# Mixer scalings by one number per row on ScalarE, all step orders written anew, table loads ahead of waits

## The reference, cut to what matters

```python
x  = L0_attn_x
xn = layernorm(x); s = L0_mixer(xn); g = silu(fp4_ffn(xn));        x = x + s * g
xn = layernorm(x); s = L1_entmax_attention(xn); g = silu(moe8(xn)); x = x + s * g
xn = layernorm(x); s = L2_rotating_recurrence(xn); g = silu(moe8_bf16(xn)); x = x + s * g
xn = layernorm(x); s = L3_relative_attention(xn); g = silu(int8_ffn(xn)); x = x + s * g
```

```python
xdt   = x * dt                       # dt: one number per token and head
Acs   = cumsum(dt * A)
Y     = (C B^T * exp(Acs_l - Acs_s)) @ xdt + exp(Acs) * C @ state
state = exp(Acs_last) * state + B^T @ (exp(Acs_last - Acs) * xdt)
y     = rmsnorm((Y + D * x) * silu(z)) @ W_out
```

## Time and profile before

| what | value |
|---|---|
| median of 3 runs | 3212.22 us (3211.52 to 3215.06) |
| the profiled execution, its span | 3209.0 us, 3.2 us below the median |
| PE / DVE / ACT / POOL busy | 74% / 79% / 51% / 18% |
| first part: 44 to 1960 us | DVE busiest |
| second part: 1962 to 2232 us | PE busiest |
| attention of layer 3: 2300 to 3121 us | PE busiest |
| table loads on ACT | 94, of 1283 ns each |

### The profile page before, as it was taken

The page is one execution under the profiler, slowest core; times in us unless marked ns, Lnnn a source line. Parts: engine busy times, 40 slices in busy tenths (PEclk is TensorE's granted clock), DMA queues, the critical chain, the costliest instruction groups (busy, mean ns, idle before and its releaser), DMA issues.

```text
span 3209.0 us, 40003 instructions
## 1 busy us (share of the span) xinstructions
PE 2383.4 (74%) x13729; PEld 1300.2 (41%) x13729; DVE 2544.2 (79%) x5554; ACT 1633.2 (51%) x3182; POOL 565.8 (18%) x610
## 2 busy tenths in 40 slices
PE   3697876967958769679674304997688898888888
PEld 1333333333333333334331101332366676666663
DVE  3386898998999999989989673887577777777764
ACT  1344436245344353353442412666587888777862
POOL 0000300302203003012030020001332323323320
PEclk9698987977978879779777655999799999999999
DMA  2001100100101001001010004200688877888751
GB/s 73 1 22 43 30 25 28 35 32 23 34 29 30 26 24 33 28 27 31 30 24 23 23 8 123 57 9 31 198 226 223 235 222 225 220 215 227 220 157 43
DMA packets 270758, 265.92 MB, mean 83 GB/s; under 512 B 15224, under 2 KB 244235, under 8 KB 268987
## 3 DMA queue, kind: packets, MB, share of 16 engines
q1 hardware_dynamic: 270554, 263.37, 28.8%
HBM read 130.48 MB, written 124.45 MB: 79 GB/s over the span
## 4 chain that ended last, share of the span: by engine, by line
DVE 41%; PE 31%; ACT 14%; issue 9%; DMA 2%; POOL 2%; SPq 1%; DVEq 0%; POOLq 0%; ACTq 0%
PE banks L2642 5%; PE banks L2688 4%; DVE t L2618 3%; DVE t L1017 2%; PE banks L2602 2%; DVE t L1169 2%; ACT L144 2%; DVE t L952 1%; ACT t L2629 1%; PE banks L1085 1%; ACT t L2553 1%; DVE t L2673 1%; DVE t L1700 1%; DVE t L1704 1%; ACT t L1395 1%
## 5 line engine op out<-in xcount | busy, mean ns | idle before, releaser
L2618 DVE CUSTOM_DVE_ANT_0 t<-banks,t 128x640 f32<-128x640 f32 (+7 forms) x512 | 377.8, 747 | 135.2 <-PE banks L2642 62.2
L2629 ACT ACTIVATE t<-t 128x640 f32<-128x640 f32 (+7 forms) x512 | 391.0, 780 | 81.3 <-DVE t L2618 80.4
L2642 PE MATMUL banks<-ident,t 128*128 128x128 f32 x2304 | 360.1, 281 | 41.6 <-DVE t L2839 14.4
L2642 PEld LDWEIGHTS banks<-ident,t 128*128 128x128 f32 x2304 | 253.8, 142 | 108.1 <-ACT t L2629 50.5
L2602 PE MATMUL banks<-t 128*128 128x512 bf16 (+3 forms) x768 | 197.3, 333 | 39.4 <-DVE t L2618 37.5
L2583 POOL TENSOR_TENSOR t<-t 128x512 f32<-128x512 f32 x96 | 122.6, 1277 | 551.1 <-DMA t<-relative_scratch 455.7
L548 POOL TENSOR_TENSOR t<-t 128x512 f32<-128x512 f32 x28 | 48.1, 1718 | 915.7 <-ACT t L520 915.7
L2673 DVE COPY t<-banks 128x512 f32<-128x512 f32 x256 | 175.6, 686 | 32.2 <-PE banks L2642 31.3
L1085 PE MATMUL banks<-t 128*128 128x512 f32 x256 | 145.0, 650 | 42.9 <-DVE t L1165 32.3
L1740 ACT ACTIVATE t<-t 128x16 f32<-128x16 f32 x256 | 82.5, 322 | 184.1 <-DVE t L1704 142.4
L1119 ACT ACTIVATE t<-banks 128x512 f32<-128x512 f32 x128 | 76.4, 597 | 195.6 <-PE banks L1085 195.4
(11 more groups left out here) (453 smaller groups left out, 5956.2 us busy)
## 6 DMA issues: line engine op xcount, KB each, us to landing
relative_scratch<-t SPq DMA_DIRECT2D x128, 512.0 KB, 3.6
t<-relative_scratch SPq DMA_DIRECT2D x128, 512.0 KB, 5.2
relative_scratch<-t SPq DMA_DIRECT2D x128, 256.0 KB, 4.1
t<-in_wmoe SPq DMA_DIRECT2D x64, 384.0 KB, 3.0
t<-cut_scratch SPq DMA_DIRECT2D x192, 64.0 KB
t<-t SPq DMA_DIRECT2D x16, 512.0 KB, 4.2
cut_scratch<-t SPq DMA_DIRECT2D x8, 768.0 KB, 4.1
z_scratch<-t SPq DMA_DIRECT2D x8, 512.0 KB, 3.1
```

Of the source, the lines that this page charges most:

```text
L2618: nc.vector.tensor_tensor_reduce(s.s[z][:, 0:n], ps[:, b0:b0 + 1 + i // 4, :].rearrange("p b n -> p (b n)")[:, 0:n], s.bias[r][:, j, WIDE ...
L2629: nc.scalar.activation(s.s[z][:, 0:n], s.s[z][:, 0:n], ACT.Exp, scale=-1.0, bias=s.least[:, z:z + 1]).then_inc(*a.mark("weights", u))
L2642: nc.tensor.transpose(ps[:, 4 + c % 2, (t - lo) * P:(t - lo + 1) * P], s.s[u % NS][:, t * P:(t + 1) * P], k.ident[:]).then_inc(*e.mark("tu ...
```

## The change: what it does, and the diff

Four things change.

1. In the mixer, three scalings leave VectorE. `xdt` becomes four ScalarE copies (one per head, 64 columns, with a factor per partition), `xdd` four more, and the decayed state four more into a new buffer `kept`; VectorE's addition then reads `kept`. ScalarE's copy of B no longer waits for VectorE, but for TensorE. TensorE waits for `gated_low` of VectorE and `xdd` of ScalarE where it waited for `xdd` of VectorE and `btok`.
2. In all stages the call that may load a table stands ahead of the wait of its activation and no longer behind it.
3. All tables of letters but `TURNS_POOL` are new: those of PE, ACT, DVE and SP for the first part, and those of PE, ACT and DVE for the second part and the attention.
4. One more buffer of 128x256.

```diff
     yield
+    k.table(LOGEXP)
     act.wait_ge(e, "var", u)
-    k.table(LOGEXP)
...
@@ mixer_pe
-            pe.wait_ge(v, "xdd", u, t)
-            pe.wait_ge(a, "btok", u, t)
+            pe.wait_ge(v, "gated_low", u, t)
+            pe.wait_ge(a, "xdd", u, t)
             mm(o, s.xdt[:, h, :], s.low[:, h, :], start=True, stop=first).then_inc(*e.mark())
...
@@ mixer_act
     for t in range(NT):
         yield
-        act.wait_ge(v, "xdt", u, t)
+        act.wait_ge(e, "turned", u, t)
         nc.scalar.copy(s.btok[:], ps[:, 0, DI0:DI0 + P]).then_inc(*a.mark("btok", u, t))
+        yield
+        for h in range(H0):
+            nc.scalar.activation(s.xdt[:, h, :], ps[:, 0, h * HP:(h + 1) * HP], ACT.Copy, scale=s.dt[:, t, h:h + 1]).then_inc(
+                *a.mark("xdt", u, t))
...
         yield
+        k.table(LOGEXP)
         act.wait_ge(a)
-        k.table(LOGEXP)
         nc.scalar.activation(s.ec, bank(ps, 2).rearrange("p (h t) -> p h t", h=H0), ACT.Exp).then_inc(*a.mark())
...
         nc.scalar.activation(s.dd[:], s.dd[:], ACT.Exp).then_inc(*a.mark("decay", u, t))
+        yield
+        act.wait_ge(a)
+        for h in range(H0):
+            nc.scalar.activation(s.xdd[:, h, :], s.xdt[:, h, :], ACT.Copy, scale=s.dd[:, h:h + 1]).then_inc(*a.mark("xdd", u, t))
+        if u:
+            yield
+            if t:
+                act.wait_ge(v, "state", u, t - 1)
+            for h in range(H0):
+                nc.scalar.activation(s.kept[:, h, :], s.state[:, t, h, :], ACT.Copy, scale=s.ec[:, h, P - 1:P]).then_inc(
+                    *a.mark("kept", u, t))
...
@@ mixer_dve
-        yield
-        dve.wait_ge(e, "turned", u, t)
-        tt(s.xdt[:], ps[:, 0, 0:DI0].rearrange("p (h q) -> p h q", h=H0), rep(s.dt[:, t, :], 2, HP), ALU.mult).then_inc(*v.mark("xdt", u, t))
...
-        tt(s.low, s.low, rep(s.gm[:], 1, H0), ALU.mult).then_inc(*v.mark())
-        tt(s.xdd[:], s.xdt[:], rep(s.dd[:], 2, HP), ALU.mult).then_inc(*v.mark("xdd", u, t))
+        tt(s.low, s.low, rep(s.gm[:], 1, H0), ALU.mult).then_inc(*v.mark("gated_low", u, t))
...
-            tt(s.state[:, t], s.state[:, t], rep(s.ec[:, :, P - 1], 2, HP), ALU.mult).then_inc(*v.mark())
-            yield
-            dve.wait_ge(v)
-            tt(s.state[:, t], s.state[:, t], new, ALU.add).then_inc(*v.mark("state", u, t))
+            dve.wait_ge(a, "kept", u, t)
+            tt(s.state[:, t], s.kept[:], new, ALU.add).then_inc(*v.mark("state", u, t))
...
 TURNS_SP = (
...
-    "wwwwwwwwbxiiittwwbwwwwxiiittbb"
+    "wwwbwbiwitwwwiwwwxwtibittixbb"
 )
...
-        s.xdt, s.xdd, s.btok = sb([P, H0, HP]), sb([P, H0, HP]), sb([P, P])
+        s.xdt, s.xdd, s.kept, s.btok = sb([P, H0, HP]), sb([P, H0, HP]), sb([P, H0, HP]), sb([P, P])
```

More of the change, by code:

```diff
@@ L731, in ffn0_act @@
         yield
+        k.table(SILU)
         act.wait_ge(e, "gate", u, t)
-        k.table(SILU)
         nc.scalar.activation(f.hid[t // 2][:, t % 2], ps[:, S0, 0:FF0], ACT.Silu).then_inc(*a.mark("silu", u, t))
@@ L2153, in readout2_act @@
     yield
+    k.table(ROOT)
     act.wait_ge(e, "var", b)
-    k.table(ROOT)
     nc.scalar.activation(s.stat[:, 0], ps[:, 1, 0:2], ACT.Sqrt, bias=k.eps5[:]).then_inc(*a.mark("root", b))
@@ L2274, in moe2_act @@
     yield
+    k.table(SIGMOID)
     act.wait_ge(e, "logits", b)
-    k.table(SIGMOID)
     nc.scalar.activation(o.rb.score, ps[:, bb, 0:NT * E2].rearrange("p (t e) -> p t e", t=NT), ACT.Sigmoid).then_inc(
```

241 lines of the change are left out of this document (120 added, 121 removed).

## The result

The changed kernel takes 3206.06 us (median of 16 runs, 3201.09 to 3212.53), the kernel before, run beside it, 3214.76 us. The ratio is 0.9965, 95% interval 0.9954 to 0.9975: faster by 0.35%, which is 8.7 us by the two medians and 11 us by the ratio. The forecast was 3160 us, a gain of 52. The sign was right, the size was not, and the range 3100 to 3222 held the time.

What follows compares the result with a forecast made beforehand. VectorE was taken as the bound, 94% busy in the first part's steady blocks. Terms -57.5 + 18 - 13 + 13 - 5 - 8 = -52.5 us against 3209.0 gave 3156.5, forecast as 3160 us, range 3100 to 3222.

Steps and rivals of the forecast that it cites:

- the order of the first part: First part: new order uses a sixth of VectorE's remaining idle time, -8 us, bounds -30 and +20.
- the relief: Mixer: three scalings leave VectorE, worth nearly their whole length, -57.5 us, with +18 coming back at once.
- the attention's 0: Second part and attention: the new sequence changes nothing, 0 us, bounds -30 and +30.
- The port wait: Mixer: two-input VectorE instructions still wait for GpSimd's product, returning +18 us, bounds 0 and 27.
- -13 for the decay wait: Mixer: VectorE's 19.7 us wait for ScalarE's exponentials shrinks behind longer cover, -13 us, bounds -20 and +14.
- +13 for the recurrence: Recurrence: its 13.1 us wait for ScalarE's small scaling, now behind mixer groups, doubles, +13 us, bounds 0 and +40.
- Loads ahead of waits: ScalarE, all stages: table loads moved ahead of waits hide some idle time, -5 us, bounds -23 and 0.
- the relief comes back as waits: Rival, first part: GpSimd, decay and recurrence waits eat the gain, leaving -3.5 us, 3209 us; chance 0.13.
- the period stayed near 215: Sign, first part: block period falls from 215 to about 208 us; staying near 215 means the relief comes back.
- ScalarE becomes a hop in every mixer step: Rival, mixer: loads, copies and queued scaling on ScalarE slow the kernel, +34.5 us, 3247 us; chance 0.15.
- The new order gains more: Rival: order also shortens idle time in fill, drain and attention, a sixth of 289 us, giving 3112 us; chance 0.20.
- the order has decided: Sign: attention or drain changing by more than 30 us would mean the order, not the scalings, decided.

Runs made afterwards that it cites:

- e18: Kernel before without scalings, with new second-part and attention orders, loads ahead of waits, first-part Silu as Relu without its table loads: ratio 0.9784, -69.4 us.
- e3: Changed kernel with two scalings (decayed inputs, state) back on VectorE: ratio 1.0091 to the kernel before, +29.2 us.
- e6: Changed kernel without the 368 ScalarE copies, so no scalings on any engine: ratio 0.9971 to the kernel before, -9.3 us.
- e5: Kernel before without the three scalings on any engine, order and loads unchanged: ratio 0.9942, -18.6 us.
- e17: Kernel before without scalings, first part in old order, second part and attention in new order, loads ahead of waits: ratio 0.9891, -35.0 us.
- e2: Kernel before with only the attention's three tables of turns from the changed kernel: ratio 0.9945, -17.7 us.
- e4: Kernel before with table loads moved ahead of their waits, order and scalings unchanged: ratio 0.9987, -4.2 us.
- e1: Kernel before with the three scalings as ScalarE copies, order and table loads unchanged: ratio 1.0129, +41.5 us.
- e10: Kernel before with every first-part Silu as Relu and its table never loaded, 61 loads less: ratio 0.9979, -6.7 us.

## Why the prediction was wrong

Two steps failed. The term for the order of the first part was -8 and measured +25.7. And the relief, -57.5 + 18 = -39.5 in the sum, measured -18.6, because half of it came back as VectorE waiting for ScalarE. A third term, the attention's 0, measured -17.7 and hid part of the miss.

**What bounds.** VectorE at 94% did set the pace, but not alone. That an instruction off VectorE "is worth nearly its whole length, as long as no new wait takes its place" is the step that failed here: the wait came. The -57.5 and +18 were nearly right as busy time (36.5 us of 39.5 under the old order), and e18 shows them worth their length where ScalarE is light. With the table loads in ScalarE's queue half of it turned into idle time, and VectorE's waits for ScalarE are what grew. I had weighed ScalarE by its busy share, 108 of 208 (it measured 109 of 216), and called it not the bound. Its queue is in order, and VectorE reads from it in every step: it limits by delay, at a share of one half. The loads are shown to decide this under the old order alone. Under the new one, with 37 more of them, two of the three scalings taken off VectorE are worth 38.5 us (e3 to e6, which also lacks the third's copies on ScalarE; 25.6 us of VectorE's busy time). So where the steps stand counts as much as how many loads there are.

**The port wait.** +18 was the estimate, 22 the size. I had looked only at what stands behind L622. Eleven times GpSimd was first and L622 itself waited, since VectorE was still at another instruction when the exponential was done. The mechanism was right, the count of places was not, and that the size came out close is in part luck.

**ScalarE's additions.** Copies took 0.23 to 0.27 us each (93 us in sum, 80.7 us of busy time against e6; I had 81). Their effect, -13 for the decay wait and +13 for the recurrence, was 0 in sum, and e6 measured 2 us, within the intervals. This agreement is luck. The decay wait moved by -2, not -13; the recurrence's by +13.4, as said, but 8 of these are there without any copy.

**Loads ahead of waits.** -5 forecast, -4.2 measured.

**The order otherwise.** This is the largest miss. I put -8 on the first part; in kernels without the scalings, the new order of that part alone costs 26 to 28. I put 0 on the attention; it gives 17.7. The first term came from idle time that an order might use and from the look of the table, the second from nothing but its bounds; neither came from a chain. The trace of before could bound them (-30 to +20, -30 to +30), and the first lay outside its bound.

In sum, from kernel to kernel: relief -18.6 (before to e5), the other orders and the loads ahead -16.4 (e5 to e17), order of the first part +25.7 (e17 to e6), copies -2.0 (e6 to changed), together -11.3. The second step measured 16.4 where e2 and e4 alone give 21.9; each step has 5 to 9 us of uncertainty.

**The rivals.** The time is the one of "the relief comes back as waits" (3209), and the sign named for it came: the period stayed near 215. Of its three parts one is there (the decay wait staying, +11 on the sum), one in part (GpSimd 22 us of 27), and the third is not (the recurrence's wait grew by 13.4, not by 40). That its time was met is luck: it has no term for the order of the first part or for the attention, and these, 25.7 and -17.7 us, are of the size of its own. "ScalarE becomes a hop in every mixer step" (3247) is what e1 measured, 3257, under the old order. It was right about the scalings under the old order and wrong about the kernel. Under the new one the copies cost nothing that shows (e6). "The new order gains more" failed for the fill and the drain: the drain has 134.3 us busy of 190.7, as before. Only the attention gave.

**The signs.** VectorE's busy time fell by 30.0 us (40 named), the period stayed, the decay wait was 17.7 us (under 10 named), the recurrence's 26.5 (26 named), and the attention moved by 20 (within 30). The sign for "the order has decided" was a change of the attention or the drain by more than 30 us. It did not come, and the order did decide: its place was the first part, where no sign looked for it.

**What stays open.** Which rows of the new first part cost the 26 us: the two waits above are where 13 of them show, not why. The tables of the engines lean on one another, and a mixture of old and new was not run. Nor is it shown what part the granted clock has in it, or which of the three attention tables gains.

## What to carry to other kernels

Do not price an edit apart from the order it runs in: the three scalings moved to ScalarE cost 41 us under one order, and under another it gained 40 to have two of them there. When the bound engine is relieved, ask first which in-order queue answers it in every step, and count what stands in that queue (loads and copies), not its busy share. Then run the parts of a joint change apart: here the part that never touched the moved work carried the gain, and the best version leaves the rest out.

## What the hardware showed that was not expected

- 61 table loads (78 us of ScalarE) were worth 6.7 us under a loaded VectorE (e10) and 34.4 under a relieved one (e17 to e18). The loads did not change, only who waited.
- When GpSimd and VectorE contend, either can lose: L622 lasts 0.69 us alone and up to 1.78 behind a product that started first; a 64-column instruction of 0.26 us lasts 1.29.
- A group of four activations of 64 columns takes 0.93 us from the banks and 1.06 from SBUF, less than the 4 x 0.33 of its single durations.
